# Cross-attention with split fp32 on one core: the value projection moved behind the keys, and work moved off and within VectorE

## The reference, cut to what matters

```python
q = split_heads(x @ Wq.T)            # 20 heads x 32
k = split_heads(ctx @ Wk.T)
v = split_heads(ctx @ Wv.T)
p = softmax(q @ k.T / sqrt(32))
out = merge_heads(p @ v) @ Wo.T + bo + x
```

## Time and profile before

| what | value |
|---|---|
| median of 3 runs | 444.74 us (444.53 to 446.11) |
| the profiled execution | 445.5 us, of which the span from first to last instruction is 443.7 us |
| PE busy | 432.1 us (97% of the span) |
| DVE busy | 314.3 us (71%) |
| ACT busy | 250.7 us (57%) |
| POOL busy | 228.2 us (51%) |
| granted TensorE clock, mean | 0.995 |

### The profile page before, as it was taken

How to read it: one execution, slowest core, us unless ns; L and a number is a source line. 1 busy time by engine, 2 the same in 40 slices (tenths; PEclk the granted TensorE clock), 3 DMA queues, 4 the chain that set the end, 5 groups by cost and what they waited for, 6 DMA issues and landing times.

```text
span 443.7 us, 8269 instructions
## 1 busy us (share of the span) xinstructions
PE 432.1 (97%) x2538; PEld 313.7 (71%) x2538; DVE 314.3 (71%) x509; ACT 250.7 (57%) x509; POOL 228.2 (51%) x184
## 2 busy tenths in 40 slices
PE   8989989899999999999999999999999999999996
PEld 6967665576777767776777766777777766777675
DVE  0465896877869586967869586967869586966663
ACT  1728876846565464756565464756565464755510
POOL 7403796836546373636546373636546373634440
PEclk9999989999999999999999999999999999999999
DMA  8995433535344534445344534455345443445203
GB/s 286 398 394 161 160 101 127 192 123 189 121 143 164 178 136 145 173 180 195 120 144 160 178 139 144 169 182 194 123 143 166 154 157 120 148 154 177 73 24 120
DMA packets 39615, 72.70 MB, mean 164 GB/s; under 512 B 5024, under 2 KB 6176, under 8 KB 39584
## 3 DMA queue, kind: packets, MB, share of 16 engines
q1 hardware_dynamic: 28784, 52.62, 33.2%
q10 hardware_dynamic: 10800, 19.67, 13.9%
HBM read 28.81 MB, written 10.49 MB: 89 GB/s over the span
## 4 chain that ended last, share of the span: by engine, by line
PE 91%; DVE 3%; ACT 2%; issue 1%; DMA 1%; POOL 1%; DVEq 0%; ACTq 0%; POOLq 0%
PE ps_q L676 30%; PE ps_o L676 26%; PE ps_s L722 9%; PE ps_pv L729 6%; PE ps_m L708 6%; PE ps_den L734 4%; PE ps_m L773 1%; DMA q_packed<-mxT 1%; PE ps_s L647 1%; PE ps_m L713 1%; PE ps_o L660 1%; PE ps_q L773 1%; ACT p_f L415 1%; PE ps_q L639 1%; DVE x_f L573 1%
## 5 line engine op out<-in xcount | busy, mean ns | idle before, releaser
L325 POOL TENSOR_TENSOR p_lo<-p_f,p_hi 77x512 f16<-77x512 f32 x120 | 147.7, 1236 | 169.6 <-ACT p_hi L419 169.6
L415 ACT ACTIVATE p_f<-ps_s 77x512 f32<-77x512 f32 x160 | 95.0, 593 | 47.4 <-PE ps_s L722 47.4
L419 ACT ACTIVATE p_hi<-ps_s 77x512 f16<-77x512 f32 x160 | 93.9, 587 | 1.0 <-PE ps_den L734 0.8
L534 DVE TENSOR_REDUCE mx<-ps_m 128x4 f32<-128x308 f32 x160 | 68.8, 471 | 18.0 <-PE ps_m L708 17.5
L676 PE MATMUL ps_q<-x_hi,wq_hi 128*128 128x512 f32 x200 | 79.9, 399 | 0.0
L676 PE MATMUL ps_q<-x_hi,wq_lo 128*128 128x512 f32 x200 | 78.5, 393 | 0.0
L676 PE MATMUL ps_q<-x_lo,wq_hi 128*128 128x512 f32 x200 | 78.5, 392 | 0.0
L527 DVE TENSOR_TENSOR q_lo<-ps_q,q_hi 128x512 fp32r<-128x512 f32 x40 | 27.6, 690 | 68.7 <-ACT q_hi L398 68.7
L398 ACT CAST q_hi<-ps_q 128x512 fp32r<-128x512 f32 x40 | 23.4, 585 | 91.8 <-PE ps_q L676 91.8
L676 PE MATMUL ps_o<-attn_hi,wo_hi 128*128 128x512 f32 x170 | 69.5, 409 | 0.0
L676 PE MATMUL ps_o<-attn_lo,wo_hi 128*128 128x512 f32 x170 | 66.9, 394 | 0.0
(11 more groups left out here) (105 smaller groups left out, 602.5 us busy)
## 6 DMA issues: line engine op xcount, KB each, us to landing
q_packed<-q_hi SPq DMA_DIRECT2D x80, 256.0 KB, 2.5
x_f<-in_x SPq DMA_DIRECT2D x40, 256.0 KB, 3.1
q_packed<-q_lo SPq DMA_DIRECT2D x40, 256.0 KB, 3.2
x_res<-in_x ACTq DMA_DIRECT2D x35, 256.0 KB, 2.8
out<-out_sb ACTq DMA_DIRECT2D x35, 256.0 KB, 2.6
wk_sb<-in_wk SPq DMA_DIRECT2D x8, 320.0 KB, 5.2
wv_sb<-in_wv SPq DMA_DIRECT2D x5, 512.0 KB, 10.9
wq_sb<-in_wq SPq DMA_DIRECT2D x5, 320.0 KB, 9.0
```

The lines of the kernel that those rows point to most:

```text
L325: nc.gpsimd.tensor_tensor(p_lo[:, i, :], p_f[:, i, :], p_hi[:, i, :], ALU.subtract).then_inc(plo_pool, 1)
L415: nc.scalar.activation(p_f[:, i, :], ps_s[i % 2][0:L, :], ACT.Exp, scale=SCALE).then_inc(pf_done, 1)
L419: nc.scalar.activation(p_hi[:, i, :], ps_s[i % 2][0:L, :], ACT.Exp, scale=SCALE).then_inc(phi_done, 1)
L534: nc.vector.tensor_reduce(mx[:, g % RS, :, tt], ps_m[tt % 2][:, 0:HG * L].rearrange("p (h k) -> p h k", k=L), AX_X, ALU.max).then_inc(max_ ...
```

## The change

The wv loads of groups 0 and 1 go ahead of wq's group 0 and x, those of groups 2 to 4 right behind x of tile 0. TensorE projects all five groups of v directly behind the keys, each into a bank of its own (ps_m0, ps_m1, ps_q, ps_o, ps_pv), with vT double buffered, and then unit (0, 0)'s queries. Query units with an odd number up to 7 go to ps_o, the others to ps_q, and for units 2 to 7 the wait on q_low is moved one unit back. The order in `fill` is changed: chunks 0 to 2 of the queries stand around the first max scores and the first scores, the transpose of the maxima stands behind the third score matmul, and the fourth score matmul behind the last chunk. ACT copies q_hi ahead of the fourth exponential there. wq_lo of groups 1 to 4 is made by POOL. In every step DVE's x_low of the first chunk stands behind reduce_max 0 and 1.

```diff
         def _(sp):
+            load_wv(0)
+            load_wv(1)
             for g in range(G):
                 sp.dma_start(wq_sb[:, g, :], wq[:, g, :]).then_inc(wq_in[g], 16)
                 if g == 0:
                     load_x(0, range(G))
+                    for v in range(2, G):
+                        load_wv(v)
                     sp.dma_start(bias[:, :], bo).then_inc(bias_in, 16)
-                sp.dma_start(wv_sb[:, g, :], wv[:, g, :]).then_inc(wv_in[g], 16)
...
+        v_banks = [ps_m[0], ps_m[1], ps_q, ps_o, ps_pv]
+        def query_bank(t, g):
+            return ps_o if isinstance(t, int) and t <= 1 and nth(t, g) < G + RS and nth(t, g) % 2 == 1 else ps_q
...
         def _(pool):                       # step
+                for c in query_group(t, g):
+                    wq_low(c)
...
         def _(act):                        # ahead of the steps
+            start_k()
             w_high(wq_in, wq_sb, wq_hi, wq_hi_done, (0,))
-            x_high(0, range(G))
-            start_k()
-            diagonal_k(0, range(HG))
+            x_high(0, range(0, 3))
+            v_high(0)
+            x_high(0, range(3, G))
+            v_high(1)
+            diagonal_k(0, range(0, 2))
+            v_high(2)
+            diagonal_k(0, range(2, HG))
+            v_high(3)
+            v_high(4)
+            w_high(wq_in, wq_sb, wq_hi, wq_hi_done, (1,))
...
         def _(act):                        # step
-                for v in value_group(t, g):
-                    v_high(v)
                 if exists(shift(t, g, 1)[0]):
                     copy_max(*shift(t, g, 1))
+                if filling(t, g):
+                    q_high(*shift(t, g, 2))
                 if exists(t):
                     exponentials(t, g, 3)
...
         def _(dve):                        # ahead of the steps
-            x_low(0, DVE_CHUNKS)
-            start_k()
+            start_k()
+            wq_low((0,))
+            scale_v(0)
+            x_low(0, DVE_CHUNKS[:1])
+            scale_v(1)
+            v_low(0)
+            x_low(0, DVE_CHUNKS[1:])
+            scale_v(2)
...
+            v_low(4)
...
         def _(dve):                        # step
-                if xt is not None:
-                    x_low(xt, DVE_CHUNKS[:1])
-                for v in value_group(t, g):
-                    scale_v(v)
                 if exists(shift(t, g, 1)[0]):
                     reduce_max(*shift(t, g, 1), 0)
                     reduce_max(*shift(t, g, 1), 1)
+                if xt is not None:
+                    x_low(xt, DVE_CHUNKS[:1])
                 if exists(t):
                     p_low(t, g, 0)
...
-                wq_low(query_group(t, g))
...
         def project_q
+                if 0 in chunks and isinstance(t, int) and 2 <= nth(t, g) < G + RS:
+                    pe.wait_ge(qlo_done, nth(t, g) - 1)
+                elif 0 in chunks and exists(shift(t, g, -1)[0]):
                     pe.wait_ge(qlo_done, nth(t, g))
...
         def fill(t, g):                    # step (-1, 3)
+                    project_v(0)
+                    project_v(1)
+                    for v in range(2, G):
+                        transpose_v(v - 2)
+                        project_v(v)
+                    transpose_v(3)
+                    pe.wait_ge(vlo_done, 3)
+                    project_q(*query, range(0, 2))
+                    transpose_v(4)
+                    project_q(*query, range(2, G))
                     return
...
+                early = query[1] != 0      # the other steps, in this order:
+                if early:
+                    project_q(*query, (0,))
+                max_scores 0, 1
+                if early:
+                    project_q(*query, (1,))
+                (0, 0) only: project_q(*query, (2,)), wait for k_packed
+                scores 0, 1
+                if early and (t, g) != (0, 0):
+                    project_q(*query, (2,))
+                values of the unit before
+                if not early:
+                    project_q(*query, (0, 1))
+                max_scores 2, 3
+                project_q(*query, (3,) if early else (2, 3))
+                scores 2
+                transpose_max
+                project_q(*query, (4,))
+                scores 3
```

More of the change, by code:

```diff
@@ L334, in _, with wq_low @@
             x_low(0, POOL_CHUNKS)
+            def wq_low(c):
+                pool.wait_ge(wq_hi_done, c + 1)
+                pool.wait_ge(wq_lo_done, c)
+                nc.gpsimd.tensor_tensor(wq_lo[:, c, :], wq_sb[:, c, :], wq_hi[:, c, :].bitcast(F32),
+                                        ALU.subtract).then_inc(wq_lo_done, 1)
             def wo_low(c):
@@ L470, in step @@
                 attn_high(at, [c for c in (4,) if c in chunks])
-                if exists(shift(t, g, 2)[0]):
+                if exists(shift(t, g, 2)[0]) and not filling(t, g):
                     q_high(*shift(t, g, 2))
@@ L503, in scale_v @@
                 dve.wait_ge(vproj_done, g + 1)
-                nc.vector.tensor_reduce(v_scale[:, g:g + 1], ps_v, AX_X, ALU.max,
+                nc.vector.tensor_reduce(v_scale[:, g:g + 1], ps_v[g], AX_X, ALU.max,
                                         apply_absolute_value=True).then_inc(vscale_done, 1)
@@ L610, in step @@
                     x_low(xt, DVE_CHUNKS[1:])
-                for v in value_group(t, g):
-                    v_low(v)
                 if exists(last_t):
@@ L652, in project_v @@
             def project_v(g):
-                if g == 0:
+                if g == RS:
                     pe.wait_ge(klo_done, G)
-                else:
-                    pe.wait_ge(vlo_done, g)
                 pe.wait_ge(wv_in[g], 16)
                 for c in range(CC):
-                    last = nc.tensor.matmul(ps_v, wv_sb[:, g, P * c:P * (c + 1)], ctx_sb[:, c, :],
+                    last = nc.tensor.matmul(ps_v[g], wv_sb[:, g, P * c:P * (c + 1)], ctx_sb[:, c, :],
                                             start=(c == 0), stop=(c == CC - 1))
@@ L694, in ready @@
                         wait_chunk(xhi_done, xlo_dve, xlo_pool, t, c)
-                if 0 in chunks and exists(shift(t, g, -1)[0]):
+                if 0 in chunks and isinstance(t, int) and 2 <= nth(t, g) < G + RS:
+                    pe.wait_ge(qlo_done, nth(t, g) - 1)
+                elif 0 in chunks and exists(shift(t, g, -1)[0]):
                     pe.wait_ge(qlo_done, nth(t, g))
-                project(ps_q, wq_hi, wq_lo, x_hi, x_lo, g, chunks, ready, q_chunks)
+                project(query_bank(t, g), wq_hi, wq_lo, x_hi, x_lo, g, chunks, ready, q_chunks)
             def max_scores(t, g, tt, b):
@@ L791, in fill @@
                 if (t, g) == (-1, G - 2):
-                    project_q(*query, range(G))
+                    project_v(0)
[8 more added lines that the diff above has]
+                    project_q(*query, range(2, G))
                     return
@@ L795, in fill @@
                     pe.wait_ge(diag_done, HG)
-                    pe.wait_ge(klo_done, G)
-                for v in value_group(t, g):
-                    project_v(v)
-                if value_group(t, g):
-                    max_scores(max_t, max_g, 0, batch(max_t))
-                    max_scores(max_t, max_g, 1, batch(max_t))
+                    pe.wait_ge(vlo_done, G - 1)
+                if (t, g) == (0, 1):
+                    pe.wait_ge(vlo_done, G)
+                early = query[1] != 0
+                if early:
+                    project_q(*query, (0,))
+                max_scores(max_t, max_g, 0, batch(max_t))
+                max_scores(max_t, max_g, 1, batch(max_t))
+                if early:
+                    project_q(*query, (1,))
                 if (t, g) == (0, 0):
+                    project_q(*query, (2,))
                     pe.wait_ge(kpack_in, 16 * 3)
@@ L807, in fill @@
                     scores(t, g, 1, batch(t))
+                if early and (t, g) != (0, 0):
+                    project_q(*query, (2,))
                 if exists(last_t):
-                    pe.wait_ge(vlo_done, nth(t, g))
                     values(last_t, last_g, batch(last_t))
-                if not value_group(t, g):
-                    max_scores(max_t, max_g, 0, batch(max_t))
-                    max_scores(max_t, max_g, 1, batch(max_t))
-                project_q(*query, (0,))
+                if not early:
+                    project_q(*query, (0, 1))
                 max_scores(max_t, max_g, 2, batch(max_t))
                 max_scores(max_t, max_g, 3, batch(max_t))
+                project_q(*query, (3,) if early else (2, 3))
                 if exists(t):
                     scores(t, g, 2, batch(t))
-                for v in value_group(t, g):
-                    transpose_v(v)
+                transpose_max(max_t, max_g)
+                project_q(*query, (4,))
                 if exists(t):
                     scores(t, g, 3, batch(t))
```

(4 more changed lines are left out.)

32 lines of the change are left out of this document (21 added, 11 removed).

## The result

The changed kernel takes **461.87 us** (median of 4 runs, 461.27 to 462.64) against 444.63 us of the kernel before on the same chip: ratio 1.0381, 95% interval 1.0354 to 1.0408. It is slower, by 17.2 us. The profiled execution took 461.85 us with a span of 460.0; the span of before is 443.7, so 16.3 us are to be found.

A forecast was written before the change was run, and what follows sets the result against it. PE was busy 97% of the span, so any added wait costs in full. To 444.74 us came +5.5 for the fill and +4.5 for the loop, making 454.7 us; range 445.5 to 462.5 (8 in 10).

The forecast's parts named there:

- The loop: Six steps that split x: the transpose of the maxima comes 0.75 us later each, +4.5 us.
- B: The main forecast: POOL's p_low goes ahead of DVE's p_low in the loop; total 454.7 us, chance 0.35.
- q_low of unit 0: Fill, ahead of unit (0, 1)'s queries: PE waits for q_low without project_v(0) as cover, +1.6 us.
- The transposes: Fill: PE waits at the transposes of the maxima for an unchanged DVE chain, 7.0 us, bounds 3.5 and 8.5.
- The maxima's DMA: Fill: the wait of 1.6 goes, three of 0.4 us come behind x and wo loads, 1.2 us, bounds 0 and 2.4.
- x of tile 1: Step (0, 2): PE waits for q_high, p_low, x_low and maxima while x is split, 2.7 us, bounds 1 and 4.
- rival C: Loop: DVE loses a second turn to POOL's x_low of chunk 4, +12 us, total 462.3, chance 0.16.
- No slow clock: Fill: no slow clock counted; a stretch like the earlier one would add 1.7 us.
- The first full step: Step (1, 1): `values` wait for p_hi and p_low of the head whose score now stands last, 2.3 us, bounds 1 and 3.
- forecast fill +5.5: Fill: waits of 15.4 us against 8.8 that go, +6.6, taken as +5.5 us, bounds +1.5 and +8.
- Rival D: DVE has the maxima ready before PE asks, so no transpose waits; total 440.0 us, chance 0.12.
- A: Loop: DVE's p_low wins the 0.04 us tie against POOL, -1.9 us, total 448.3, chance 0.27.

The follow-up runs named there:

- e1_loop_only: Kernel before with only DVE's x_low of chunk 1 moved behind reduce_max 0 and 1 in steps that split x; 449.69 us.
- e7_unit1_no_wait: Kernel after without the wait of unit 1's first query chunk on q_low of unit 0; 461.18 us.
- e3_pool_yields: Kernel after with POOL waiting in step (0, 2) for DVE's x_low of chunks 1 and 3 between its own three x_low; 455.96 us.
- e12_pool_last_too: Kernel before with both of DVE's x_low behind all four maxima and POOL's last x_low between its p_low of heads 2 and 3; 441.81 us.
- e6_score_first: Kernel after with score 3 ahead of the last query chunk in step (1, 0) and ACT's q_high behind the last exponential; 462.68 us.
- e9_chunk1_first: Kernel before with ACT making x_high of chunk 1 ahead of chunk 0 in steps that split x; 448.08 us.
- e10_gaps: Kernel after with a tiny POOL memset ahead of each of its three x_low of step (0, 2) and one behind the last; 463.43 us.
- e5_chunk_behind: Kernel after with one query chunk of each fill step moved from ahead of `values` to behind the second pair of max scores; 461.06 us.
- e4_wq_on_pool: Kernel before with only wq_low of groups 1 to 4 made on POOL instead of DVE; 449.85 us.
- e11_yields_old_loop: Kernel after with DVE's x_low of chunk 1 ahead of the maxima again and POOL giving DVE two turns in step (0, 2); 451.24 us.
- e8_x_low_last: Kernel before with both of DVE's x_low of a step behind all four maxima; 444.89 us.

## Why the prediction was right, and where it wasn't

The sign is right, and so is it that both parts lose, the fill and the loop; 454.7 us was 7.2 us too low, within the range of 445.5 to 462.5.

- **The loop, +4.5.** Exact: 5.10 forecast as 5.1, DVE's p_low 1.67 forecast as 1.7, and e1_loop_only shows it alone. That is B. The shared turn in the earlier trace rows was the right precedent.
- **q_low of unit 0, +1.6.** The wait is 1.62. Its price was less: without it the queries of unit 1 start only 0.6 us earlier (e7_unit1_no_wait), because wq_low on POOL comes next, so "wq_low costs nothing" was also wrong, by a wait of 0.75 that q_low hid. That term was a wait, not its worth.
- **The transposes, 7.0.** With 0.16 added to each the waits are 1.2 in (0, 0), 0.95 in (0, 1), (0, 4) and (1, 0), 1.6 in (0, 2): 5.7, and about 0.3 in (-1, 4), 6.0 in all. Right in place and mechanism.
- **The maxima's DMA, 1.2.** 0.6 + 0.3 measured.
- **x of tile 1, 2.7: the step that failed.** The wait for q_high was right (0.44 + 0.16, forecast 0.6), the one for x_high of 0.62 had no term. DVE's x_low was put at 1.15 and was 3.59 + 0.16. I let DVE lose one turn; it lost four, and took 5.9 us for one subtraction. The row at 111.10 in the earlier trace rows, which I used for rival C, had said that more than one turn can be lost; I priced it in the loop and not here, where three x_low and a wo_low of POOL follow one another.
- **No slow clock.** That was the second miss. Waits of 2.7 and 2.3 us stood in my own sum, and the earlier trace rows shows half clock behind less than that. It cost 2.6 us in the stretch of (0, 4) by e3_pool_yields. A second stretch behind the wait of 2.03 stands from 94 to 101 us; how much it costs alone I couldn't separate (the whole step (1, 1) is 1.1 us longer: 12.59 from `values` to `values` against 11.48). And the stretch of before, which the sum takes away at 1.7 us, was worth 0.8: its step from (0, 3) to (0, 4) takes 9.83 us, against 9.05 in e1_loop_only and 9.04 in e12_pool_last_too, which have no slow clock there.
- **The first full step, 2.3.** 2.2 measured, but for another reason than the one I gave, as e6_score_first shows: ACT's queue. It may also be why moving v away loses anywhere, which no run tests alone: at the end of the fill ACT sets 6.7 us from `values` to `values`, and v's matmuls were work that PE had beside such a chain.

By sizes: forecast fill +5.5, measured +11.75. 2.6 more for x_low and 2.6 for the clock behind it make 10.7. Of the other 1.05, 0.9 is the stretch of before that was counted too high; the smaller misses (0.8 for x_high, 1.1 for step (1, 1), 1.0 less for the transposes) partly offset each other, and the 1.1 that I took off the sum for shorter waits was a guess that no row gave. The bound of +8 was too low by x_low and the clock. Rival D is refuted by the eleven waits, A and C by the distance of 5.1. The total came out near C's 462.3 by chance: C's mechanism didn't happen, the extra time was lost in the fill. And it was C that drew the range up to 462.5, so the range holds the result by luck too.

The Trainium skill, "SBUF — State Buffer", section "Who interferes with whom", gave the same sum for the loop as the rows did, and the loop came out so. For the x_low of step (0, 2) its rule that issue order decides would let DVE, which waited from 63.96, in ahead of POOL's x_low of 64.10, or at the latest behind it at 65.4, and so end by 66; the trace has 63.96 + 5.93 = 69.9. The trace doesn't agree with the rule there, and what decides instead is open.

## What to carry to other kernels

Work that you take out of a step because it seems to be in the way may be the cover of that step's longest chain: ask, for each engine, how long the step is without it. When DVE and POOL both subtract two SBUF tensors, count as a bound the turns that DVE can lose until POOL next has to stop, and put POOL's semaphore wait where DVE has its critical pair; here that, with both x_low behind the maxima, was worth 3.2 us, and the x_low behind the maxima alone nothing. And put a term for the slow clock behind a long PE wait, with a range: here it was 2.6 us behind the wait of 3.6, at most 1.1 behind the wait of 2.0 in after, and nothing behind one of 2.1 at 32 us in e9_chunk1_first.

## What the hardware showed

**Turns between DVE and POOL.** A DVE subtraction that gets its turn ends 0.56 us behind POOL's instruction; without POOL it takes 0.68. In all these traces DVE got in when POOL's next instruction was waiting for a semaphore or was a p_low. When it was an x_low, attn_low or wo_low whose input was ready, DVE could lose the turn, one after the other up to four times, but didn't always: in after DVE's p_low of 121.65 went ahead of POOL's x_low of 122.73, and in before DVE's x_low of 60.36 went ahead of an x_low of POOL shown from 61.54. A p_low has up to three semaphore waits ahead of it in the code, the others one, and it covers 77 partitions with f16 output instead of 128. What decides wasn't tried; e10_gaps shows only that an instruction of 0.1 us in between doesn't let DVE in.

**The slow clock.** The granted clock fell to 0.50, the 1.2 GHz level, behind PE waits of 2.0 (94 us), 2.2 (e5_chunk_behind, 57 us), 3.6 (70 us) and 4.1 us (e4_wq_on_pool, 56 us), each time for 6 to 7 us. It doesn't follow from the length of the wait: in e11_yields_old_loop the same wait of 2.0 had half clock only from 91 to 94.5 us, and at the wait for the first maxima's DMA e8_x_low_last (2.4 us) and e4_wq_on_pool (1.8 us) had it from 34 to 37 us, and e9_chunk1_first (2.1 us) not at all. In the kernels built from before, the short stretch of the earlier trace rows isn't always there: windows from 60 to 70 us of e12_pool_last_too all show 1.00. Where it is, it costs 0.8 us (9.83 against 9.05). Differences of about 1 us between profiled executions in the fill are therefore not to be explained by an edit.
